# Phase 1 and 2 of a fused attention and ternary FFN kernel: key transposes moved inside the tile, scan of |W| on three buffers

## The chip, the cores and the metric

One Trainium2 chip, eight NeuronCores, one program. The time is device microseconds of the slowest core. Each core owns 8 of the 32 query tiles of one batch element (cores 0 to 3 the first, 4 to 7 the second), and computes keys and values for all 32 tiles of its batch element itself. No core talks to another.

## The reference, cut to what is computed

```python
xn = layernorm(x)                                    # x: [2, 4096, 2048] f32
q, k, v = xn @ Wq.T, xn @ Wk.T, xn @ Wv.T            # 16 heads of 128
q = LN_head(q * gamma + beta) * 128**-0.5            # layernorm over each head
k = LN_head(k * gamma + beta)
attn = tril((q @ k.T) ** 2)
o = (attn @ v) / (attn.sum(-1) + 1e-5)
attn_out = o @ Wo.T
# FFN with ternary weights and int8 activations
wq(w) = clip(round(w / m), -1, 1) * m,  m = mean(|w|)      # over the whole matrix
gate, up = bit_linear(xn, gate_w).split(2)           # gate_w [11264, 2048]
ffn = bit_linear(silu(gate) * up, down_w)            # down_w [2048, 5632]
return x + attn_out + ffn
```

The mean of |w| over each whole FFN matrix is needed before any weight can be made ternary. The kernel gets it by reading both matrices once in 264 chunks of 128x1024 float32 (512 KB) beside the attention's projections; this text calls it the scan.

## The kernel before, in words

The program is written as five in-order instruction lists, one for each engine: `sync` (SP, most DMAs), `gpsimd` (POOL, the casting weight loads and the scan's loads), `tensor` (PE), `vector` (DVE) and `scalar` (ACT). Nothing reorders them: the order in which the Python code calls the helpers is the order in each queue, and an instruction whose semaphore isn't there holds everything behind it on its engine.

**Phase 1** (`for t in range(NT)`, 32 tiles of 128 tokens) makes keys and values. For tile t:
- `pe_transposes` (L339): 16 transposes of the normalized tile `xnb` into two PSUM banks `tp_ps`, four to a bank, copied to `xnT` by ACT (groups 0 and 2, L345) and DVE (1 and 3, L349). The third group needs the bank that ACT's first copy frees.
- `proj_mm(wk_sb)` and `proj_mm(wv_sb)` (L364): 64 matmuls each into the same four banks `kv_ps`, so the V projection can only start in a bank when DVE has read K from it.
- `head_transposes_store` (L418): 16 transposes of the finished keys `kfm`, copied by ACT (L425) and DVE (L429) into two small buffers `ktb` (they are `sgn[0]` and `sgn[1]`; `sgn` in the rows), and stored to `ksc` in 16 DMAs of 32 KB on SP (256 bytes per partition). Groups 2 and 3 wait until the four stores of groups 0 and 1 have landed. Here it is the keys of tile **t-1** that are transposed and stored, between the K and V projections of tile t: `kfm` and `kfm2` form a ring.
- `featuremap_evac` (L374, DVE: K times gamma, PSUM to `kg`), `ln_tile` of tile t+1 (L299 to L322), `featuremap` (L381 to L402: beta, per-head layernorm, ends with 16 small DVE instructions that write `kfm`).
- four ACT copies of V (L480) and 16 stores to `vsc`.
- `emit_abs` (the scan, L283 on ACT, buffer `wfp`): two chunks before the V copies and four after the V stores, so that on ACT six stand together, broken only by the V copies. The load of a chunk is a POOL DMA that waits until the ACT instruction that last read its buffer is done. There are two buffers.
The load of the next tile, `xf`, is on SP, behind the stores of the tile before.

**Phase 2** (`for s in range(NOWN)`, 8 own tiles) makes queries and the int8 activations in the same manner, with 3+3+3 chunks of the scan in each tile. `head_transposes_store` is called twice, for the queries (`qsc`, 16 DMAs of 32 KB) and for the quantized activations (`xqsc`, through `wide_fn`: 4 DMAs of 128 KB, 1024 bytes per partition). Here the keys' ring is already used: tile s-1 is stored after the projection of tile s. Ahead of the next K projection DVE has to get through the quantization (L552 to L573), which starts when ACT's L549 is done; L549 stands behind three chunks of the scan.

**Phase 3** is the attention, and behind it, in the same stretch between barriers, `emit_thresh` turns the sums of the scan into thresholds (L700 to L728, a chain of small DVE and PE instructions). **Phase 4** is the output projection and the FFN. Between phases all engines meet at a barrier.

## Time and profile before

| what | value |
|---|---|
| median of the timed runs | 5087.8 us (5084.0 and 5091.6) |
| profiled execution | 5106.7 us, span of its slowest core 5105.2 us |
| cores of that execution | 5045.9 to 5105.2 us, granted TensorE clock 0.818 to 0.824 of full |
| start until the first projection | 0 to 114 us |
| phase 1 | 114 to 2001 us |
| phase 2 | 2001 to 2592 us |
| phase 3, attention | 2592 to 3543 us |
| thresholds | 3543 to 3551 us |
| phase 4 | 3551 to 5105 us |

Times in the rows are microseconds from the span's start. In a view in order of time a row has the start, the time the group of like instructions took, engine, line, output<-inputs and count; in brackets is how long the engine had been idle and what released it. TensorE's clock is at 1.2 GHz or at 2.4 GHz; the granted clock of a stretch is the mean share of 2.4 GHz.

### The profile page before, as it was taken

The numbers are of one execution on the slowest core, as the hardware profiler recorded it, in microseconds if no ns is written. First come the engines' busy times: TensorE is split into PE (matmuls) and PEld (weight loads), VectorE is DVE, ScalarE is ACT, GpSimd is POOL, SyncE is SP. The second block draws the span as 40 slices with busy tenths as digits, with TensorE's granted clock in tenths as the row PEclk, the third lists the DMA queues.
The fourth block names the chain that finished last, engine by engine and source line by source line (L and its number), as shares of the span: only waits on it lengthen the run. The fifth ranks groups of instructions, "written<-read, shape, count | busy, mean of one in ns | idle before, by whom it ended". The sixth has DMA issues, their size and how long they took to land.

```text
span 5105.2 us, 52147 instructions; the slowest of 8 cores (5045.9 to 5105.2 us)
## 1 busy us (share of the span) xinstructions
PE 3066.7 (60%) x13416; PEld 1270.3 (25%) x13416; DVE 1845.7 (36%) x3416; ACT 1816.3 (36%) x2685; POOL 240.6 (5%) x452
## 2 busy tenths in 40 slices
PE   1665556655556563233346667776889999512789
PEld 0222222222222221111111112221334433201333
DVE  0333333333433342444433312222266666333221
ACT  0222222222322222222334455554144444354551
POOL 1000000000000001000000000000000000000000
PEclk9777777777877876666679899999999999755899
DMA  9333332232233225433221221111466666345886
GB/s 165 83 83 88 92 104 85 83 87 83 88 105 92 85 84 127 113 99 107 91 88 47 56 87 59 65 71 51 120 234 229 232 236 225 122 160 170 248 277 201
DMA packets 312716, 628.19 MB, mean 123 GB/s; under 512 B 181872, under 2 KB 194160, under 8 KB 280432
## 3 DMA queue, kind: packets, MB, share of 16 engines
q0 software_dynamic: 64512, 310.41, 20.2%
q1 hardware_dynamic: 247920, 314.45, 19.9%
q8 instruction: 123, 2.02, 0.2%
q14 instruction: 161, 1.32, 0.1%
HBM read 573.34 MB, written 84.93 MB: 129 GB/s over the span
## 4 chain that ended last, share of the span: by engine, by line
PE 28%; DVE 22%; DMA 18%; ACT 14%; issue 11%; SPq 3%; another core or an unknown queue 2%; DVEq 1%; ACTq 1%; POOLq 0%; POOL 0%
PE kv_ps L364 13%; DMA wfp<-gwt_r 6%; DMA xob<-xown 4%; PE ops L675 3%; SPq L80 3%; ACT s2t L658 3%; DVE s2t L660 2%; DMA hgr<-hgscr 2%; ACT sgn L762 2%; ACT sgn L765 2%; PE zps L679 2%; PE sps L647 2%; PE dps L1138 2%; DVE kg L381 2%
## 5 line engine op out<-in xcount | busy, mean ns | idle before, releaser
L364 PE MATMUL kv_ps<-wk_sb,xnT 128*128 128x512 bf16 x2560 | 644.3, 419 | 159.9 <-DMA wv_sb<-wvt 84.8
L364 PE MATMUL kv_ps<-wv_sb,xnT 128*128 128x512 bf16 x2048 | 517.3, 420 | 176.2 <-DVE kg L374 176.2
L339 PE MATMUL tp_ps<-ident,xnb 128*128 128x128 bf16 x640 | 69.5, 272 | 835.3 <-ACT xnT L345 691.4
L675 PE MATMUL ops<-s2t,vsb 128*128 128x512 bf16 x768 | 302.4, 394 | 285.1 <-DVE s2t L660 233.3
L660 DVE TENSOR_TENSOR s2t<-s2t,msk_sb 128x512 bf16<-128x512 bf16 x512 | 217.3, 424 | 630.0 <-ACT s2t L658 625.4
L658 ACT ACTIVATE s2t<-sps 128x512 bf16<-128x512 f32 x512 | 305.8, 597 | 316.8 <-PE sps L647 306.3
L283 ACT ACTIVATE sgn<-wfp 128x1024 bf16<-128x1024 f32 x264 | 279.1, 1057 | 343.7 <-DMA wfp<-gwt_r 190.5
L364 PEld LDWEIGHTS kv_ps<-wk_sb,xnT 128*128 128x128 bf16 x2560 | 267.4, 106 | 527.8 <-issue 284.1
L913 PE MATMUL gps<-terng,xqs 128*128 128x512 bf16 x1408 | 343.8, 401 | 74.0 <-DVE ternu L781 57.4
L1138 PE MATMUL dps<-dtern,hqts 128*128 128x512 bf16 x1408 | 330.7, 398 | 72.9 <-DMA hqts<-hqtd 66.4
L425 ACT COPY sgn<-tp_ps 128x512 bf16<-128x512 bf16 x96 | 56.3, 586 | 793.3 <-PE tp_ps L418 621.2
L364 PEld LDWEIGHTS kv_ps<-wv_sb,xnT 128*128 128x128 bf16 x2048 | 214.9, 106 | 468.5 <-issue 274.5
L429 DVE COPY sgn<-tp_ps 128x512 bf16<-128x512 bf16 x96 | 40.8, 425 | 782.7 <-PE tp_ps L418 532.0
L647 PE MATMUL sps<-qsb,ksb 128*128 128x512 bf16 x768 | 303.4, 397 | 28.5 <-DMA qsb<-qsc 28.4
L925 PE MATMUL ups<-ternu,xqs 128*128 128x512 bf16 x1408 | 318.3, 379 | 0.0
L679 PE MATMUL zps<-s2t,ones_bf 128*128 128x512 bf16 x768 | 304.2, 396 | 0.0
L339 PEld LDWEIGHTS tp_ps<-ident,xnb 128*128 128x128 bf16 x640 | 51.7, 121 | 860.0 <-issue 860.0
L675 PEld LDWEIGHTS ops<-s2t,vsb 128*128 128x128 bf16 x768 | 74.5, 97 | 560.4 <-issue 559.1
L913 PEld LDWEIGHTS gps<-terng,xqs 128*128 128x128 bf16 x1408 | 143.2, 102 | 262.1 <-issue 113.2
L374 DVE TENSOR_TENSOR kg<-kv_ps,gmb 128x512 f32<-128x512 f32 x160 | 110.7, 692 | 268.1 <-PE kv_ps L364 235.9
L1138 PEld LDWEIGHTS dps<-dtern,hqts 128*128 128x128 bf16 x1408 | 141.3, 102 | 262.0 <-issue 115.0
L1066 PE MATMUL tp<-ident,hgb 128*128 128x128 bf16 x352 | 51.5, 301 | 244.3 <-DVE hgb L1042 173.9
(138 smaller groups left out, 3542.3 us busy)
## 6 DMA issues: line engine op xcount, KB each, us to landing
wfp<-gwt_r POOLq DMA_DIRECT2D x176, 512.0 KB, 4.9
wfpt<-gwt_r POOLq DMA_DIRECT2D x88, 1024.0 KB, 5.2
wfp<-dwt_r POOLq DMA_DIRECT2D x88, 512.0 KB, 4.2
xqs<-xqsc SPq DMA_DIRECT2D x88, 512.0 KB, 3.9
wfpt<-dwt_r POOLq DMA_DIRECT2D x44, 1024.0 KB, 8.0
hqts<-hqtd SPq DMA_DIRECT2D x32, 1408.0 KB, 8.9
xf<-xfull SPq DMA_DIRECT2D x32, 1024.0 KB, 7.1
hgscr<-hgb SPq DMA_DIRECT2D x88, 256.0 KB, 2.1
```

What stands on the lines that cost most here:

```text
L80: return self.op(engine, lambda e, o=out, i=in_: e.dma_start(out=o, in_=i), waits=waits, inc=sem, inc_n=16)
L283: lambda e, sl=slot, t=tgt, cc=col: e.activation(wabs_dump[:], wfp[sl][:], ACT.Abs, accum_out=t[:, cc:cc + 1]), waits=[s_abs[slot]]))
L339: TE(lambda e, bb=bank, f=fc, jj=j, s=src_bf: e.transpose(bb[:, jj * 128:(jj + 1) * 128], s[:, f * 128:(f + 1) * 128], ident[:]), waits=wl ...
L364: TE(lambda e, jj=j, f=fc, w=w_sb: e.matmul(kv_ps[jj][:], xnT[:, f * 128:(f + 1) * 128], w[:, f * DM + jj * 512: f * DM + (jj + 1) * 512], ...
L647: TE(lambda e, sl=slot, vv=v, bb=sb: e.matmul(sps[bb][:], ksb[sl][:, vv * 128:(vv + 1) * 128], qsb[sl][:], start=True, stop=True), waits=w ...
L658: sck = SC(lambda e, bb=sb: e.activation(s2t[bb][:], sps[bb][:], ACT.Square), waits=[(cT, mm_ck)])
L660: vck = V(lambda e, bb=sb, vv=v: e.tensor_tensor(s2t[bb][:], s2t[bb][:], msk_sb[:, (vv % 16) * 512:((vv % 16) + 1) * 512], ALU.mult), wait ...
L675: TE(lambda e, sl=slot, vv=v, bb=sb, hh=h, n=NC: e.matmul(ops_[hh % 2][:], vsb[sl][:, vv * 128:(vv + 1) * 128], s2t[bb][:], start=(vv == 0 ...
L679: TE(lambda e, vv=v, bb=sb, hh=h, n=NC: e.matmul(zps[hh % 2][:], ones_bf[:], s2t[bb][:], start=(vv == 0), stop=(vv == n - 1)), inc=(v == N ...
L913: TE(lambda e, f=fc, r=ring, bb=pb, xs=xslot: e.matmul(gps[bb][:], xqs[xs][:, f * 128:(f + 1) * 128], terng[r][:, f * 512:(f + 1) * 512], ...
L925: TE(lambda e, f=fc, r=ring, bb=pb, xs=xslot: e.matmul(ups[bb][:], xqs[xs][:, f * 128:(f + 1) * 128], ternu[r][:, f * 512:(f + 1) * 512], ...
L1138: TE(lambda e, f=fc, h_=hs, bb=pb, r=ring: e.matmul(dps[bb][:], hqts[h_][:, f * 128:(f + 1) * 128], dtern[r][:, f * 512:(f + 1) * 512], st ...
```

## The change

1. In phase 1 the keys of tile t are transposed and stored in iteration t itself: behind the V projection, `ln_tile` and `featuremap`, ahead of the V copies. `kfm2` is not used in phase 1 any more.
2. The scan has three buffers `wfp` instead of two, and its six chunks of a tile stand in three pairs: behind the copies to `xnT`, behind `featuremap`, and behind the V stores. In phase 2 the places are as before.
3. The stores of the quantized activations in phase 2 are 16 DMAs of 32 KB instead of 4 of 128 KB. The layout in DRAM is the same.
4. The thresholds are computed behind phase 2, between two barriers, instead of behind the attention.
5. Every one of the 16 V stores has its wait written out; `lnz` is in another buffer; an unused semaphore and an unused branch go.

```diff
-    wfp = [E(nc.sbuf_tensor(f"wfp{i}", [128, 1024], F32)) for i in range(2)]
+    wfp = [E(nc.sbuf_tensor(f"wfp{i}", [128, 1024], F32)) for i in range(3)]
-    lnz = kg
+    lnz = wfp[0]
...
-            slot = i % 2
+            slot = i % 3
...
         kck = proj_mm(wk_sb, first_waits=[(s_w, ck_winit)] + xnT_ready)
-        if pend1[0] is not None:
-            pfm = pend1[0]
-            head_transposes_store(kfm_ring[(t - 1) % 2], pfm,
-                                  lambda h, tt=t - 1: ksc[h, :, tt, :])
-            kfm_free2[(t - 1) % 2] = [(cT, cT.n)]
+        emit_abs(2)
         featuremap_evac(kck)
         vck_banks = proj_mm(wv_sb, first_waits=[])
...
-        fm_ck = featuremap(kfm_ring[slot], q_scale=False,
-                           dst_waits=kfm_free2[slot])
-        pend1[0] = fm_ck
+        fm_ck = featuremap(kfm, q_scale=False,
+                           dst_waits=st["kfm_free"])
         emit_abs(2)
+        kt_ck = head_transposes_store(kfm, fm_ck,
+                                      lambda h, tt=t: ksc[h, :, tt, :])
+        st["kfm_free"] = [(cT, kt_ck)]
         for j in range(4):
             v = SC(lambda e, jj=j, xs=slot: e.copy(
...
-                  s_kvw[slot], waits=([(cS, sck)] if h == 0 else []))
+                  s_kvw[slot], waits=[(cS, sck)])
         st["xnb_free"][slot] = [(s_kvw[slot], s_kvw[slot].n)]
         emit_abs(2)
-        emit_abs(2)
-    head_transposes_store(kfm_ring[(NT - 1) % 2], pend1[0],
-                          lambda h: ksc[h, :, NT - 1, :])
...
-            head_transposes_store(xnb[pslot], pqb, None,
-                                  wide_fn=lambda g, ss=s - 1:
-                                  xqsc[ss].rearrange("p f c -> p (f c)")
-                                  [:, g * 512:(g + 1) * 512])
+            head_transposes_store(xnb[pslot], pqb,
+                                  lambda fc, ss=s - 1: xqsc[ss, :, fc, :])
...
     b.wait("sync", s_ktb[0], s_ktb[1], s_kvw[0], s_kvw[1])
+    b.barrier(bar)
+    emit_thresh(wabs_g, N_GW, thg_p, thg_m, hmg, 176)
+    emit_thresh(wabs_d, N_DW, thd_p, thd_m, hmd, 88)
...
     b.barrier(bar)
```

The order of TensorE in phase 1 before, from one K projection on (`kfm` are the keys to be transposed, `xnb` the normalized tile):

```order
L364 MATMUL kv_ps<-wk_sb,xnT 128x512 x64
L418 MATMUL tp_ps<-ident,kfm 128x128 x16
L364 MATMUL kv_ps<-wv_sb,xnT 128x512 x64
L339 MATMUL tp_ps<-ident,xnb 128x128 x16
L364 MATMUL kv_ps<-wk_sb,xnT 128x512 x64
```

and with the change:

```order
L354 MATMUL kv_ps<-wk_sb,xnT 128x512 x64
L354 MATMUL kv_ps<-wv_sb,xnT 128x512 x64
L408 MATMUL tp_ps<-ident,kfm 128x128 x16
L329 MATMUL tp_ps<-ident,xnb 128x128 x16
L354 MATMUL kv_ps<-wk_sb,xnT 128x512 x64
```

The transposes of the keys moved from between the two projections to behind them, and are now those of the same tile. The order of ScalarE in phase 1 before, from the end of one tile's feature map on (`sgn<-wfp` is the scan, `xnb<-kv_ps` the V copies, `sgn<-tp_ps` the copies of transposed keys):

```order
L395 ACTIVATE st<-st 128x16
L283 ACTIVATE sgn,wabs_g<-wfp 128x1024 x2
L480 CAST xnb<-kv_ps 128x512 x4
L283 ACTIVATE sgn,wabs_g<-wfp 128x1024 x4
L345 COPY xnT<-tp_ps 128x512 x2
L425 COPY sgn<-tp_ps 128x512 x2
L299 ACTIVATE xnb,lnst<-xf 128x2048
```

and with the change:

```order
L385 ACTIVATE st<-st 128x16
L273 ACTIVATE sgn,wabs_g<-wfp 128x1024 x2
L415 COPY sgn<-tp_ps 128x512 x2
L459 CAST xnb<-kv_ps 128x512 x4
L273 ACTIVATE sgn,wabs_g<-wfp 128x1024 x2
L335 COPY xnT<-tp_ps 128x512 x2
L273 ACTIVATE sgn,wabs_g<-wfp 128x1024 x2
L289 ACTIVATE xnb,lnst<-xf 128x2048
```

Of the four chunks between the V copies and the copies to `xnT` two stay, and two now stand behind the copies to `xnT`.

## Rows read from the trace of the kernel before

**Rows 1.** The stretches of the program, busy time of each engine (first row: columns).

```profile
core 5: us, PE busy (x) PEld busy (x) DVE busy (x) ACT busy (x) POOL busy (x), PEclk, DMA share, GB/s
...
114.00:2001.00 1887.00, 1116.13 (x5104) 499.14 (x5104) 663.14 (x1239) 504.08 (x793) 102.27 (x190) 0.79 0.31 88
2001.00:2592.50 591.50, 175.51 (x896) 84.67 (x896) 259.62 (x432) 163.21 (x256) 48.30 (x88) 0.62 0.39 109
...
3543.00:3552.00 9.00, 1.48 (x8) 1.22 (x8) 3.27 (x20) 0.00 (x0) 0.92 (x2) 0.53 0.00 1
```

**Rows 2.** Who waited for whom from 160 to 1960 us: us, times, longest.

```profile
PE tp_ps L339 <- ACT xnT L345: 513.1, 31, 20.8
...
ACT sgn L283 <- DMA wfp<-gwt_r: 188.4, 111, 7.0
PE kv_ps L364 <- DVE kg L374: 170.5, 30, 6.1
```

**Rows 3.** TensorE in order of time, one tile of phase 1 from K to K.

```profile
1003.02 16.11 PE L364 MATMUL kv_ps<-wk_sb,xnT 128*128 128x512 bf16 x64 [0.96 <-DVE xnT L349]
...
1026.53 16.30 PE L364 MATMUL kv_ps<-wv_sb,xnT 128*128 128x512 bf16 x64 [5.63 <-DVE kg L374]
...
1061.70 1.87 PE L364 MATMUL kv_ps<-wk_sb,xnT 128*128 128x512 bf16 x4 [0.96 <-DVE xnT L349]
```

**Rows 4.** ScalarE in order of time, the same tile.

```profile
1019.55 0.59 ACT L425 COPY sgn<-tp_ps 128x512 bf16<-128x512 bf16 x1 [17.18 <-PE tp_ps L418]
1023.24 0.59 ACT L425 COPY sgn<-tp_ps 128x512 bf16<-128x512 bf16 x1 [3.10 <-DMA ksc<-sgn]
...
1045.58 2.60 ACT L480 CAST xnb<-kv_ps 128x512 bf16<-128x512 f32 x4
...
1057.77 1.06 ACT L283 ACTIVATE sgn<-wfp 128x1024 bf16<-128x1024 f32 x1 [2.36 <-DMA wfp<-gwt_r]
...
1059.01 0.59 ACT L345 COPY xnT<-tp_ps 128x512 bf16<-128x512 bf16 x1
```

**Rows 5.** VectorE in order of time, the same tile.

```profile
1028.87 2.29 DVE L302 TENSOR_REDUCE lnst<-xf 128x1 f32<-128x2048 f32 x1
...
1034.44 2.29 DVE L381 TENSOR_TENSOR kg<-kg,btb 128x2048 f32<-128x2048 f32 x1
...
1043.53 4.19 DVE L402 TENSOR_SCALAR kfm<-kg,st 128x128 bf16<-128x128 f32 x16
```

**Rows 6.** TensorE in order of time, tile 0.

```profile
113.98 16.88 PE L364 MATMUL kv_ps<-wk_sb,xnT 128*128 128x512 bf16 x64 [84.75 <-DMA wv_sb<-wvt]
130.70 13.98 PE L364 MATMUL kv_ps<-wv_sb,xnT 128*128 128x512 bf16 x64
```

**Rows 7.** VectorE in order of time, tile 0, the row behind the last read of K.

```profile
131.92 2.29 DVE L302 TENSOR_REDUCE lnst<-xf 128x1 f32<-128x2048 f32 x1
```

**Rows 8.** SP's queue in order of time, the tile of rows 3.

```profile
1020.21 7.41 SPq L80 DMA_DIRECT2D ksc<-sgn  x16
1048.25 7.92 SPq L80 DMA_DIRECT2D vsc<-xnb  x16
1056.32 0.43 SPq L80 DMA_DIRECT2D xf<-xfull  x1
```

**Rows 9.** DMA issues of phase 1: count, KB each, median us to landing.

```profile
wfp<-gwt_r POOLq DMA_DIRECT2D x170, 512.0 KB, 4.9
...
ksc<-sgn SPq DMA_DIRECT2D x496, 32.0 KB, 1.5
vsc<-xnb SPq DMA_DIRECT2D x496, 32.0 KB, 3.0
```

**Rows 10.** Phase 2, all engines in order of time, behind one tile's feature map.

```profile
2344.46 4.41 SPq L80 DMA_DIRECT2D xqsc<-sgn  x4
...
2364.96 4.19 DVE L402 TENSOR_SCALAR kfm<-kg,st 128x128 bf16<-128x128 f32 x16
...
2370.39 1.06 ACT L283 ACTIVATE sgn<-wfp 128x1024 bf16<-128x1024 f32 x1 [3.75 <-DMA wfp<-dwt_r]
...
2371.63 1.91 ACT L549 ACTIVATE kg<-xn_f 128x2048 f32<-128x2048 f32 x1
...
2373.80 0.15 DVE L552 TENSOR_SCALAR lnst<-lnst 128x1 f32<-128x1 f32 x1 [4.65 <-ACT kg L549]
```

More of the change, by code:

```diff
@@ L270, in emit_abs @@
             src, which, col = abs_chunks[i]
[L271 to L272 removed]
+            slot = i % 3
             b.dma("gpsimd", wfp[slot][:], src, s_abs[slot],
[L274 removed]
+                  waits=[(cS, abs_sc_ck[slot])])
             tgt = wabs_g if which == 0 else wabs_d
[L276 to L285 removed]
+            abs_sc_ck[slot] = SC(
+                lambda e, sl=slot, t=tgt, cc=col: e.activation(
+                    wabs_dump[:], wfp[sl][:], ACT.Abs,
+                    accum_out=t[:, cc:cc + 1]), waits=[s_abs[slot]])
     st = {
@@ L433, in head_transposes_store @@
             st["tp_evac"][g % 2] = ck
-            if wide_fn is not None:
-                b.dma("sync", wide_fn(g), ktb[kslot][:, 0:512],
+            for j in range(4):
+                h = g * 4 + j
+                b.dma("sync", dst_fn(h), ktb[kslot][:, j * 128:(j + 1) * 128],
                       s_ktb[kslot], waits=[(CTR[ck[0]], ck[1])])
-            else:
-                for j in range(4):
-                    h = g * 4 + j
-                    b.dma("sync", dst_fn(h), ktb[kslot][:, j * 128:(j + 1) * 128],
-                          s_ktb[kslot], waits=[(CTR[ck[0]], ck[1])])
             st["ktb_free"][kslot] = s_ktb[kslot].n
@@ L446, in build_nc @@
     st["xn_ck"][0] = ln_tile(xf[0], want_f32=False, xslot=0)
-    kfm_ring = [kfm, kfm2]
-    kfm_free2 = [[], []]
-    pend1 = [None]
     for t in range(NT):
@@ L516, in build_nc @@
     pend = [None]
+    kfm_ring = [kfm, kfm2]
+    kfm_free2 = [list(st["kfm_free"]), []]
     for s in range(NOWN):
@@ new lines, in build_nc, with emit_thresh @@
+    assert abs_i[0] == len(abs_chunks), abs_i[0]
+    def emit_thresh(src, n_elems, th_p, th_m, hm, ncols):
+        ngr = ncols // 11
+        V(lambda e, s_=src, ng=ngr: e.reduce_sum(
+            wabs_r.ap()[:, 0:ng].rearrange("p (g o) -> p g o", o=1),
+            s_.ap().rearrange("p (g d) -> p g d", g=ng), axis=AX.X),
+          waits=[(cS, cS.n)])
+        V(lambda e, ng=ngr: e.reduce_sum(wabs_s[:, 0:1], wabs_r[:, 0:ng], axis=AX.X))
+        TE(lambda e: e.matmul(minips[0:1, 0:1], wabs_s[:], onesrf[:],
+                              start=True, stop=True), waits=[(cV, cV.n)])
+        tck = cT.n
+        V(lambda e: e.tensor_copy(mini1[0:1, 0:1], minips[0:1, 0:1]),
+          waits=[(cT, tck)])
+        V(lambda e, n=n_elems: e.tensor_single_scalar(
+            mini1[0:1, 1:2], mini1[0:1, 0:1], 1.0 / n, ALU.mult))
+        V(lambda e: e.tensor_single_scalar(mini1[0:1, 1:2], mini1[0:1, 1:2],
+                                           EPS, ALU.max))
+        vck = V(lambda e: e.tensor_single_scalar(mini1[0:1, 2:3], mini1[0:1, 1:2],
+                                                 0.5, ALU.mult))
+        TE(lambda e: e.matmul(minips[:, 0:2], ones1f[:], mini1[0:1, 1:3],
+                              start=True, stop=True), waits=[(cV, vck)])
+        tck = cT.n
+        V(lambda e, hh=hm: e.tensor_single_scalar(hh[:], minips[:, 0:1], 0.5,
+                                                  ALU.mult), waits=[(cT, tck)])
+        V(lambda e, tp=th_p: e.tensor_copy(tp[:], minips[:, 1:2]))
+        vck = V(lambda e, tm=th_m: e.tensor_single_scalar(
+            tm[:], minips[:, 1:2], -1.0, ALU.mult))
+        return vck
```

65 lines of the change are left out of this document (10 added, 55 removed).

## The prediction

> **What bounds the kernel now.** I read the stretches first [rows 1]. Phase 1 is 1887 of 5105 us, 59 us for each of 32 tiles, with a granted clock of 0.79 and 30% DMA share: TensorE is busy 1116 us and waits the rest. Phase 2 is another 591.5 us, the thresholds stand alone in 9 us. The change touches nothing else. Next, who waited for whom in phase 1 [rows 2]: TensorE loses 513 us in 31 waits (16.5 us a tile) for ScalarE's copy to `xnT`, and 170.5 us in 30 waits (5.7 us a tile) for VectorE's read of K. ScalarE itself waits for scan loads, 188 us in 111 waits, 1.7 us each.
>
> Then one tile in order of time. K runs from 1003.02, V from 1026.53, the next K from 1061.70, a period of 58.7 us [rows 3]. The first hole lies between K and V: the transposes of the old keys stand there, and their last copy on VectorE waits for stores, with the reads of K queued behind it, so V starts 7.4 us after K's end (1019.13 to 1026.53). The second lies behind V's end at 1042.83: ScalarE has two scan chunks, the V copies (1045.58), four more chunks, of which the last begins at 1057.77 after waiting 2.36 us for its load, and only then the copy at 1059.01 that frees the bank for the third group of transposes. K follows 2.69 us later [rows 3, 4]. With two buffers and four chunks in a row, ScalarE runs at the pace of the loads.
>
> **Part 1 and 2, phase 1, worked out as one new tile.** Time 0 is the start of K. The queues are in order, so the new period is a chain whose links I take from the old rows.
> - K takes 16.1 us [rows 3]. V follows at once, since nothing holds VectorE's reads of K now. Tile 0 of before already has that order, as there are no old keys to transpose: V's row has no wait, and takes 13.98 us, not 16.30, because TensorE doesn't fall back to the lower clock between them [rows 3, 6]. V ends at 30.1.
> - VectorE begins the layernorm of the next tile 1.06 us after K's end (130.86 to 131.92) [rows 6, 7]: at 17.2.
> - From there to the end of `kfm` it is 18.85 us (1028.87 to 1047.72) [rows 5]: 36.0. V is hidden under this; TensorE waits 5.9 us.
> - The first group is transposed and ScalarE begins to copy it about 0.85 us later. (An estimate: the 2.69 us from copy to K hold two such steps and two copies, of 0.59 and some 0.4.) 36.9. The scan pair ahead of it takes 2 x 1.24 us (1057.77 to 1059.01 is one) from about 31 on, and is done.
> - The copy of the third group starts 3.69 us behind the first (1019.55 to 1023.24, with 3.10 us of waiting for the stores) [rows 4] and takes 0.6: 41.2.
> - V copies 2.6: 43.8. Scan pair 2.5: 46.4. Both its loads could start as soon as the first pair of this tile and the second one's first chunk were done, over 10 us earlier, against a landing of 4.9 us [rows 9]; so its wait goes. Then 2.7 from the copy to K: **49.1 us**.
> - VectorE's copy of the fourth group comes 1.6 us behind ScalarE's third, at 42.5, and holds nothing: the transposes behind it have until 46.4.
> - The first pair of scan chunks, behind the copies to `xnT`, lies under K, where ScalarE has nothing else.
> - SP: its 16 key stores take 7.41 us, the V stores 7.92, the load of `xf` follows [rows 8]. That puts `xf` 3.5 us into the next tile, needed at 17.2: covered by 13.7 us. The waits written out at the V stores cost nothing, the key stores have the same kind and are issued no slower.
>
> What is new is that the key stores go out while the two loads just asked for by the second pair may still be moving. Rows bound this: key stores land in 1.5 us when alone, V stores, which share their time with scan loads, in 3.0 [rows 9]. So each tile may pay 0 to 1.5 us at the third group. Most of the loads are over by then (asked for at about 33 and 34, landing in 4.9), so I take 0.5: 49.6 us. The Trainium skill ("Trainium Kernel Development and Optimization", Key Constraints) says that DMAs of SP and POOL run on the same 16 engines and interleave. The landing times of rows 9 agree with it; by that rule alone the upper end, 1.5 us, would hold, some 30 us on the total.
>
> Tile 0 has a K of 16.9: 50.4. The last tile has no layernorm of a next one (5.6 us less, 1028.87 to 1034.44 [rows 5]), and ends on SP: keys out at 16.1 + 1.1 + 13.3 + 0.85 + 0.6 = 31.9, then 7.4 and 7.9 of stores and 0.5 for contention: 48. Sum 50.4 + 30 x 49.6 + 48 = 1586 against 1887 [rows 1]: **-301 us**.
>
> **Part 2 and 3, phase 2.** Between feature map and quantization ScalarE has three scan chunks, and the third waits 3.75 us for its load [rows 10]. With three buffers all three were loaded long before. VectorE's L552 would start 3.5 us earlier, since `kfm` ends at 2369.15 and ScalarE's L549 takes 2.1; this chain sets the next K. The stores go against it: 16 of 32 KB are issued at the pace of rows 8, 0.46 us each, 1.85 for a group of four, 7.4 for all, where the four wide ones take 4.4 [rows 8, 10]. The next layernorm is queued behind the last of those copies on VectorE. The copies of the four groups then come 1.9 us apart; from the old order I get 1.4 us more until the last. Bounds: 0 (all hidden) and 3.0 (the whole difference). Net -2.1 a tile for six tiles, -3.5 for the first, which stores nothing, and about nothing for the last, where the stores end the phase: **-16 us**. The Trainium skill ("DMA: Bandwidth & Descriptors", Specifications) says that transfers below 512 bytes are done by read-modify-write. The stores of 256 bytes per partition in rows 9 land in 1.5 us, so I see no such price in the trace. If each of the four groups paid another 1.5 us for it, phase 2 would come out at about +20 instead of -16.
>
> **Part 4 and 5.** The threshold chain is 9 us, alone on the chip before [rows 1] and alone after, since a barrier stands on both sides. One barrier more: no row shows one by itself, between 0 and 2 us, I take 1. The other edits move nothing that anyone waits for.
>
> **Sum.** The profiled execution took 5106.7 us, 1.5 beyond its span. 5106.7 - 301 - 16 + 1 = 4790.7. It is 18.9 us above the median of the timed runs (5087.8), which I take off: **4772 us**, 6.2% less.
>
> **The rivals.**
> - *Contention eats a part.* Key stores land in 3.0 us, and the third scan pair still waits 1.7 us for each load as in rows 2. That is 1.0 + 3.4 = 4.4 us more a tile, 31 x 4.4 = 136: 4908. For it: more bytes in less time, 88 GB/s become 105. Against: before, the DMA engines stand idle through most of K and V.
> - *Slower: ScalarE's queue starves the copies.* All that TensorE needs at a tile's end now hangs on one chain with scan chunks in it. If loads issued beside 32 small stores took so long that each chunk of the third pair waited the 7.0 us that rows 2 have as their longest, the period would grow by 14: 4772 + 31 x 14 = 5206. It breaks even at 10.2 us a tile. Against: the loads are asked for over 10 us ahead.
> - *`xf` late.* It stands behind 32 stores on SP. If it landed after 24 rather than 10 us, the layernorm would hold VectorE 7 to 8 us a tile: about 5010.
> - *The clock.* TensorE is idle or at small transposes for 19 us before each K. Before it was as long (1042.83 to 1061.70), and K began at the lower clock as well (4 matmuls in 1.87 us) [rows 3]. If all of K ran so (0.43 us each, 27.5 us), 31 x 11.4 gives 5125. The trace has no such K.
>
> **How the numbers follow.** Forecast 0.80 (4735 to 4850 by itself), contention 0.12, late `xf` 0.03, starving 0.03, clock 0.02. What a measurement of this kernel can tell from no change is about 2%, 4986 to 5190. Faster 0.92, same 0.05, slower 0.03. The range of 8 in 10 runs from 4725, where the period is 48, to 4885, which takes in the full 1.5 us of contention, the bounds of phase 2 and a part of the first rival.
>
> **What would show each step.** Phase 1 of about 1586 us; K to K near 49.5; V without a wait before it and near 14 us; TensorE waiting some 6 us for `kfm` and no longer for K's reads; no scan chunk behind the V copies waiting for its load; `xf` landed before VectorE is free for it; phase 2 some 16 us shorter, its copies behind `xqsc` 1.9 us apart; the threshold chain at 9 us before the attention. The prediction is wrong if the third scan pair waits for loads, if the copies of keys wait over 5 us for their stores, or if something other than `kfm` releases the key transposes.

## The result, and the profile after

The kernel with the change takes 4803.8 us (median of 11 runs, 4786.0 to 4920.0) against 5092.9 us before, timed in turns with it (10 runs, 5079.7 to 5158.3). The ratio is 0.943, with an interval of 0.9396 to 0.9465. The forecast was 4772 us, a ratio of 0.938 to its own median. The profiled execution took 4816.7 us; its slowest core is core 2 with a span of 4815.1, where the working of the forecast, before its last step to the median, gave 4790.7. In several executions one die shows a lower granted clock than the other and all its cores are longer; these are left out of the ratios and of the medians in the table of experiments.

First the cores, then the stretches of core 2, as in [rows 1].

```profile
core 0: 4783.3 us, clock 0.814
core 1: 4799.2 us, clock 0.816
core 2: 4815.1 us, clock 0.813
...
core 5: 4784.6 us, clock 0.826
core 6: 4754.9 us, clock 0.828
```

```profile
core 2: us, PE busy (x) PEld busy (x) DVE busy (x) ACT busy (x) POOL busy (x), PEclk, DMA share, GB/s
115.10:1705.60 1590.50, 1078.75 (x5009) 509.90 (x5104) 663.15 (x1239) 505.92 (x795) 101.98 (x189) 0.79 0.38 104
1705.60:2291.70 586.10, 170.47 (x889) 85.17 (x904) 263.04 (x452) 163.16 (x256) 48.51 (x88) 0.62 0.40 110
2283.90:2291.70 7.80, 1.48 (x8) 1.22 (x8) 3.39 (x20) 0.00 (x0) 0.00 (x0) 0.50 0.00 0
```

Nearly the whole gain is in the first row: phase 1 went from 1887 us [rows 1] to 1590.5. VectorE and ScalarE do the same work as before (663.15 and 506 us); TensorE waits less, and its busy time falls a little (to 1089 us on core 5; on core 2 some 95 of its records are missing). The second row holds phase 2 and now the thresholds too: 578.3 and 7.8 us, where they were 591.5 and about 8.2.

Core for core it can be set out fully. Core 5, on which the rows of before were read, went from 5105.2 to 4784.6 us, 320.6 less, where the forecast had 316 (301 + 16 - 1). That is 296.6 in phase 1, 13.0 in phase 2 with the thresholds, 1.3 in the attention and 10.4 in phase 4, less 0.7 in the time until the first K. Phase 4 has the same instructions in both kernels; on core 2 it took 12 us *more* than on core 5 before (1566.5 against 1554.2), with a granted clock of 0.81 for 0.85.

Who waited for whom in phase 1 after the change, 160 to 1690 us (us, times, longest):

```profile
ACT xnb L289 <- DMA xf<-xfull: 308.1, 30, 11.8
...
PE tp_ps L408 <- DVE kfm L392: 192.4, 31, 6.7
...
DVE sgn L419 <- DMA ksc<-sgn: 159.9, 30, 7.0
...
ACT sgn L415 <- DMA ksc<-sgn: 102.1, 30, 4.7
...
PE tp_ps L329 <- ACT xnT L335: 98.3, 31, 3.7
PE tp_ps L329 <- ACT sgn L415: 89.1, 30, 4.2
...
PE tp_ps L329 <- DVE sgn L419: 45.0, 30, 3.1
...
ACT sgn L273 <- DMA wfp<-gwt_r: 27.8, 29, 2.3
```

Against [rows 2]: TensorE's wait for the copy to `xnT` fell from 513.1 to 98.3 us, its wait for VectorE's read of K is no longer in the list, and ScalarE's wait for scan loads fell from 188.4 to 27.8. In their place stand 192.4 us for `kfm`, 6.2 a tile, and 89.1 and 45.0 us for the two copies of keys (`sgn`, L415 and L419) that free the banks for the transposes of `xnb`: a part of the old wait for `xnT` now has other names. All waits of TensorE in these two lists add up to 747 us before and 481 after, and that difference of 265, with some 27 us less busy time, is nearly all of the gain of phase 1. The first row is long but ends before anybody needs its result: `xnb` here is only the sum of squares' scratch, and VectorE is not yet free for the next layernorm.

TensorE in order of time, one tile from K to K, to be held against [rows 3]:

```profile
1012.17 16.47 PE L354 MATMUL kv_ps<-wk_sb,xnT 128*128 128x512 bf16 x62 [1.34 <-DVE xnT L339]
...
1028.47 13.98 PE L354 MATMUL kv_ps<-wv_sb,xnT 128*128 128x512 bf16 x63
...
1049.14 1.01 PE L408 MATMUL tp_ps<-ident,kfm 128*128 128x128 bf16 x8 [6.69 <-DVE kfm L392]
...
1063.41 3.19 PE L354 MATMUL kv_ps<-wk_sb,xnT 128*128 128x512 bf16 x7 [1.34 <-DVE xnT L339]
```

V has no bracket, so it waits for nothing, and takes 13.98 us instead of 16.30. The hole is now in one piece, behind V, and is released by `kfm`.

ScalarE and VectorE of the same tile, for [rows 4, 5]; the last row is the `xnT` copy that frees the bank for the third group:

```profile
1029.68 2.29 DVE L292 TENSOR_REDUCE lnst<-xf 128x1 f32<-128x2048 f32 x1
...
1044.70 4.19 DVE L392 TENSOR_SCALAR kfm<-kg,st 128x128 bf16<-128x128 f32 x16
...
1049.92 0.59 ACT L415 COPY sgn<-tp_ps 128x512 bf16<-128x512 bf16 x1 [3.28 <-PE tp_ps L408]
...
1054.49 0.59 ACT L415 COPY sgn<-tp_ps 128x512 bf16<-128x512 bf16 x1 [3.98 <-DMA ksc<-sgn]
...
1055.16 2.60 ACT L459 CAST xnb<-kv_ps 128x512 bf16<-128x512 f32 x4
...
1057.11 0.42 DVE L419 COPY sgn<-tp_ps 128x512 bf16<-128x512 bf16 x1 [6.30 <-DMA ksc<-sgn]
...
1057.86 1.06 ACT L273 ACTIVATE sgn<-wfp 128x1024 bf16<-128x1024 f32 x1
...
1059.10 1.06 ACT L273 ACTIVATE sgn<-wfp 128x1024 bf16<-128x1024 f32 x1
...
1060.33 0.59 ACT L335 COPY xnT<-tp_ps 128x512 bf16<-128x512 bf16 x1
```

Counted from K's start at 1012.17, the links are: layernorm 17.5 (forecast 17.2), end of `kfm` 36.7 (36.0), first key copy 37.8 (36.9), third key copy 42.3 (36.9 + 3.7, with 0.5 for contention 41.1), V copies 43.0, third pair of scan chunks 45.7 (43.8 + 0.5) and without a wait, the `xnT` copy 48.2 (46.4 + 0.5), next K 51.2. VectorE's fourth key copy comes at 44.9, where the forecast had 42.5. This tile is one of the longer ones: the mean from K to K is 49.8 us, the range 48.6 to 51.4, and the forecast 49.6.

The DMA issues of phase 1, for [rows 9], and one tile of SP's queue, for [rows 8]:

```profile
wfp<-gwt_r POOLq DMA_DIRECT2D x173, 512.0 KB, 5.0
xf<-xfull SPq DMA_DIRECT2D x30, 1024.0 KB, 8.0
ksc<-sgn SPq DMA_DIRECT2D x512, 32.0 KB, 1.5
vsc<-xnb SPq DMA_DIRECT2D x511, 32.0 KB, 4.2
```

```profile
1050.58 8.78 SPq L80 DMA_DIRECT2D ksc<-sgn  x16
...
1059.45 7.33 SPq L80 DMA_DIRECT2D vsc<-xnb  x14
```

Key stores still land in 1.5 us, V stores in 4.2 where they took 3.0. `xf` lands in 8.0 us and its queue position is as late as forecast: it was asked for at 1015.54 and was there at 1025.71, 4 us before VectorE is free for it.

Phase 2 behind one tile's feature map, for [rows 10]:

```profile
1912.80 7.75 SPq L80 DMA_DIRECT2D xqsc<-sgn  x16
...
1936.88 1.06 ACT L273 ACTIVATE sgn<-wfp 128x1024 bf16<-128x1024 f32 x1
...
1938.13 1.91 ACT L525 ACTIVATE kg<-xn_f 128x2048 f32<-128x2048 f32 x1
...
1940.30 0.15 DVE L528 TENSOR_SCALAR lnst<-lnst 128x1 f32<-128x1 f32 x1 [0.99 <-ACT kg L525]
```

The third chunk has no bracket: its wait of 3.75 us is gone, and VectorE's L528 stands idle for 0.99 us instead of 4.65. The stores of the activations take 7.75 us in the queue for 4.41, and the four copies behind them (1912.15 to 1917.97) stand 1.9 us apart in the mean, as forecast.

### The profile page after: what moved, and what is told of

Its sections match the earlier page's. It is cut to its first block, busy times and chain, and to the rows that moved or that the text cites. A ratio compares the mean times of both kernels' runs of the same rounds, so it can differ in the third digit from the quotient of the medians.

```text
span 4815.1 us, 52576 instructions; the slowest of 8 cores (4754.9 to 4815.1 us)
## 1 busy us (share of the span) xinstructions
PE 3051.7 (63%) x13164; PEld 1292.5 (27%) x13416; DVE 1846.2 (38%) x3416; ACT 1815.5 (38%) x2685; POOL 241.3 (5%) x452
## 4 chain that ended last, share of the span: by engine, by line
PE 33%; DVE 24%; ACT 15%; issue 11%; DMA 10%; another core or an unknown queue 3%; SPq 3%; DVEq 1%; ACTq 1%; POOL 0%; POOLq 0%
PE kv_ps L354 13%; PE dps L1114 4%; PE ops L685 3%; ACT s2t L668 3%; DVE kfm L392 3%; SPq L80 3%; PE gps L889 3%; DMA hgr<-hgscr 2%; DVE s2t L670 2%; PE sps L657 2%; DMA xob<-xown 2%; PE zps L689 2%; ACT sgn L738 2%; ACT sgn L741 2%
## 5 line engine op out<-in xcount | busy, mean ns | idle before, releaser
L354 PE MATMUL kv_ps<-wk_sb,xnT 128*128 128x512 bf16 x2482 | 629.9, 418 | 182.2 <-DMA wv_sb<-wvt 86.2
L354 PE MATMUL kv_ps<-wv_sb,xnT 128*128 128x512 bf16 x2016 | 445.6, 379 | 1.7
L329 PE MATMUL tp_ps<-ident,xnb 128*128 128x128 bf16 x640 | 86.9, 303 | 540.7 <-ACT xnT L335 234.8
L1114 PE MATMUL dps<-dtern,hqts 128*128 128x512 bf16 x1379 | 370.1, 437 | 36.5 <-DMA hqts<-hqtd 27.8
L354 PEld LDWEIGHTS kv_ps<-wv_sb,xnT 128*128 128x128 bf16 x2048 | 200.4, 98 | 241.6
L408 PE MATMUL tp_ps<-ident,kfm 128*128 128x128 bf16 x640 | 76.0, 289 | 248.5 <-DVE kfm L392 215.7
L1114 PEld LDWEIGHTS dps<-dtern,hqts 128*128 128x128 bf16 x1408 | 152.4, 109 | 253.8 <-issue 238.4
L415 ACT COPY sgn<-tp_ps 128x512 bf16<-128x512 bf16 x96 | 56.3, 586 | 412.9 <-PE tp_ps L408 221.2
```

The lines of the kernel that those rows point to most:

```text
L329: TE(lambda e, bb=bank, f=fc, jj=j, s=src_bf: e.transpose(bb[:, jj * 128:(jj + 1) * 128], s[:, f * 128:(f + 1) * 128], ident[:]), waits=wl ...
L354: TE(lambda e, jj=j, f=fc, w=w_sb: e.matmul(kv_ps[jj][:], xnT[:, f * 128:(f + 1) * 128], w[:, f * DM + jj * 512: f * DM + (jj + 1) * 512], ...
L1114: TE(lambda e, f=fc, h_=hs, bb=pb, r=ring: e.matmul(dps[bb][:], hqts[h_][:, f * 128:(f + 1) * 128], dtern[r][:, f * 512:(f + 1) * 512], st ...
```

## The experiments

Twelve runs were made. The lengths of phase 1 and of phase 2 with the thresholds, from the profiled execution of each (the time from the first K to the load of `gnw_s`, and from there to the load of the attention's mask), are the finest measure, since the phases are apart. They are those of the core that ended last, unless the table says otherwise; K to K is the mean from tile 1 on:

| kernel | phase 1 | phase 2 + thresholds | K to K, phase 1 | median, ratio to before in the same session |
|---|---|---|---|---|
| before (core 5) | 1887.1 | 599.7 | 59.1 | 1 |
| after (core 2) | 1590.5 | 586.1 | 49.8 | 4797.8, 0.943 [0.940, 0.947] |
| two_bufs | 1634.6, low clock; 1589.1 on core 4 | 638.6, low clock | 49.6 on core 4 | 4834.5, 0.943 [0.936, 0.950] |
| tail_four | 1754.5 | 585.8 | 55.0 | 4957.3, one run |
| old_order_spread | 1685.1 | 592.8 (no thresholds) | 52.9 | 4897.7, 0.956 [0.949, 0.963] |
| no_scan_p1 | 1537.3, low clock; 1515.9 on core 0 | 587.8 | 47.4 on core 0 | 4745.7, one run |
| wide_stores | 1592.4 | 579.2 | | 4785.3, one run |
| four_slots | 1528.5 | 564.2 | 47.8 | 4722.4, 0.914 [0.907, 0.922] |
| keys_one_later | 1274.1 | 588.5 | 39.4 | 4487.4, 0.868 [0.863, 0.874] |
| two_bufs_again | 1589.6 | 616.0 | 49.8 | 4826.0, 0.942 [0.934, 0.950] |
| after_again | 1586.4 | 585.4 | 49.7 | 4799.4, 0.938 [0.932, 0.944] |
| keys_later_p2 | 1382.7, low clock | 552.8 | 38.7 to 44.4 | 4560.8, 0.888 [0.881, 0.896] |

The kernels wide_stores, four_slots and keys_one_later were timed on a chip on which at least one die had a clock of 0.78 to 0.81 in all seven executions of before (median 5163.5 us; 5114 to 5121 us in the other three sessions of experiments). Against 5117 us their ratios would be 0.923 for four_slots and 0.877 for keys_one_later. The last two runs, keys_later_same and keys_later_p2_same, stand in a table of their own further down.

### What the third scan buffer does

Everything as in the changed kernel, but with two buffers.

```diff
-    wfp = [E(nc.sbuf_tensor(f"wfp{i}", [128, 1024], F32)) for i in range(3)]
+    wfp = [E(nc.sbuf_tensor(f"wfp{i}", [128, 1024], F32)) for i in range(2)]
-            slot = i % 3
+            slot = i % 2
```

> The changed kernel with two scan buffers instead of three. Theory P (the spread into pairs does the work, not the third buffer): the third pair's loads are asked for when the second pair is done, some 9 us before they are needed, against a landing of 5, so K to K in phase 1 stays at 49.5 to 50.2 us and phase 1 at 1590 us, within 20. In phase 2 three chunks stand together and the third waits again: 2 to 3.5 us more in each of 7 tiles, so phase 2 is 15 to 22 us longer and the total about 0.947 of the kernel before. Theory B (the third buffer is needed): the chunks of the third pair wait 1.7 to 3 us each for their loads, K to K 53 to 56 us, phase 1 over 1690 us, total 0.965 to 0.985 of before.

The ratio of 0.943 is the changed kernel's own. But the profiled execution fell on a low granted clock on all cores over the whole span (0.775 to 0.793), on its slowest core with K at 18.4 us and V at 16.98 from tile 13 on, so most of its stretches can't be compared. Phase 1 of cores 4 and 5 can: their V took 13.98 us in 31 of 32 tiles, and phase 1 1589.1 and 1595.3 us, as with three buffers. The kernel was run again beside the changed kernel on one chip:

> The changed kernel with two scan buffers once more, beside the changed kernel itself on the same chip, since the first look at it ran at a lower TensorE clock throughout. Theory P (third buffer not needed where the chunks stand in pairs): K to K in phase 1 within 0.7 us of the changed kernel's 49.9, K to K in phase 2 up from 64.9 by 2 to 4 us (three chunks together), total 15 to 28 us above the changed kernel. Theory B (it is needed): phase 1 longer by 50 us or more.

> The changed kernel unaltered, to compare the one with two buffers with it on one chip: 0.943 of before as measured, within 0.005.

Phase 1 took 1589.6 us with two buffers and 1586.4 with three; phase 2 with the thresholds 616.0 and 585.4. The waits of phase 2 say where, first with two buffers, then with three:

```profile
ACT sgn L273 <- DMA wfp<-dwt_r: 129.5, 40, 44.0
```

```profile
ACT sgn L273 <- DMA wfp<-dwt_r: 62.3, 23, 45.5
```

In phase 1 ScalarE waits more often for loads as well (92.5 us in 58 waits against 19.3 in 29), but at the pair that lies under K, where nobody waits for it. So the third buffer pays only where three chunks stand together: 31 us in phase 2 between these two cores, 27 in the mean of the eight (613.3 and 586.2), 3.3 a tile, and 27 between the medians. The forecast had written "with two buffers and four chunks in a row, ScalarE runs at the pace of the loads"; the cure for phase 1 was that there are no longer four in a row, not the buffer.

### Which of the two moves makes the gain of phase 1

The order of the change is kept, and the pair that lies under K goes back behind the V stores, so that four chunks stand in the tail:

```diff
         kck = proj_mm(wk_sb, first_waits=[(s_w, ck_winit)] + xnT_ready)
-        emit_abs(2)
...
-        emit_abs(2)
+        emit_abs(4)
```

> The changed kernel, three buffers, but the first pair of scan chunks is moved back, so that four chunks stand between the V copies and the copies to xnT. Theory P: three of the four are loaded ahead (3 x 1.24 us); the fourth's load is asked for only when the first of them is done, and lands 4.9 us later. The copy to xnT comes at about 52 instead of 46.4 us into the tile, K to K 55 us, phase 1 some 170 us longer (1760 us), total 4960 to 4985 us. Theory B (with three buffers the place doesn't matter, only the chunk's own time counts): 2 x 1.24 = 2.5 us more, K to K 52.3 us, phase 1 1667 us.

Phase 1 took 1754.5 us, 55.0 from K to K in the mean (53.9 to 57.7). Two chunks moved out of the tail are worth 164 us, 5.3 a tile: twice 1.24 us of work, and the load for which the fourth chunk waits. In this kernel ScalarE's wait for loads is 78.1 us in 25 waits up to 1500 us, 3.1 each, where the changed kernel has 1.0, and that under K.

The opposite: the kernel of before, with its keys between K and V, its two buffers and wide stores, and only the scan spread into pairs.

```diff
         kck = proj_mm(wk_sb, first_waits=[(s_w, ck_winit)] + xnT_ready)
+        emit_abs(2)
         if pend1[0] is not None:
...
         emit_abs(2)
-        emit_abs(2)
```

> The kernel before with one edit: two of the four scan chunks behind the V copies now stand behind the copies to xnT of the next tile, under K. Two buffers, keys of tile t-1 still transposed between K and V. Theory P: the copy to xnT now waits for two chunks only, which by the old rows run at 1048.51 and 1051.19, so it comes at 1052.5 instead of 1059.01: K to K 52 us instead of 58.7, phase 1 about 1680 us, total 0.960 of before. So two thirds and more of the gain without moving a transpose. Theory O (the order of the transposes is what gains, the holes around V): no more than 2 us a tile, total above 0.985 of before.

Phase 1 took 1685.1 us, 202 of the 297 us of the whole change; in the mean of the eight cores it is 1874 before, 1679 here and 1588 in after_again, that is 195 of 286. So the order of the transposes is worth the other 91 to 95 us, 3 a tile (the third buffer also differs, but is worth nothing in phase 1, as shown above): V starts 7.4 us earlier and is 2.3 us shorter, but the transposes and copies of the keys, some 7 us, now stand in the tail. Taken the other way round, with tail_four (1751 in the mean of its cores) as the step between, the order gives 123 us and the spread of the scan 163: the split depends on which comes first, but the spread is the larger part either way. Phase 2 without the thresholds is 592.8, as before.

### What the scan costs in the tail

The chunks of phase 1 are left out altogether, that is 192 of the 264, so the mean of |W| is taken over too little:

```diff
             slot = i % 3
+            if i < 192:
+                continue
             b.dma("gpsimd", wfp[slot][:], src, s_abs[slot],
```

> The changed kernel without the 192 scan chunks of phase 1, loads and sums both (the thresholds come out of the 72 others). It shows what the scan still costs in phase 1. By my sum only the third pair lies on the chain, 2 x 1.24 us, and contention of its loads with the key stores and xf 0.5 us: K to K 46.6 us, phase 1 about 1495 us. If contention costs more than I took, K to K falls below 46; the key stores' wait at ScalarE's third copy is then clearly under the 3.1 to 4 us of the changed kernel, and xf lands in under 7 us instead of 8 to 10. If the scan were hidden altogether, K to K would stay at 49.7.

On core 4, the last to end, phase 1 took 1537.3 us, 53 less than after. But there and on core 5 the clock was low at first: V took 16.98 us in nine of the first ten tiles and 16.0 in the other. On the six other cores V took 13.98 us in every tile, and phase 1 1512.1 to 1518.4 us. Against the 1588 us of after_again on the same chip that is 72 less, 2.3 us a tile, where I had expected 3.0: 2.5 for the third pair's own time and 0.5 for contention. Most of what is missing is the contention, which is smaller than I took (below). The rows in order of time, from core 4 in a tile with V at 13.98 us, show a part of the rest:

```profile
1032.80 0.59 ACT L417 COPY sgn<-tp_ps 128x512 bf16<-128x512 bf16 x1 [3.08 <-DMA ksc<-sgn]
1033.47 2.61 ACT L461 CAST xnb<-kv_ps 128x512 bf16<-128x512 f32 x4
...
1036.16 0.59 ACT L337 COPY xnT<-tp_ps 128x512 bf16<-128x512 bf16 x1
1036.24 0.42 DVE L421 COPY sgn<-tp_ps 128x512 bf16<-128x512 bf16 x1 [6.21 <-DMA ksc<-sgn]
...
1036.81 1.01 PE L331 MATMUL tp_ps<-ident,xnb 128*128 128x128 bf16 x8 [2.70 <-DVE sgn L421]
```

ScalarE's `xnT` copy now comes straight behind the V copies, but VectorE's copy of the fourth key group waits 6.21 us for its stores, and the transposes of the next tile stand behind it. I had written that this copy "holds nothing". It holds nothing as long as the scan pair is there: in the tile of the changed kernel shown above the transposes behind it were done 2.8 us before those that wait for `xnT`. Without the pair they run together, in some tiles, and that can cost some tenths of a microsecond, not more, since the whole shortfall is 0.7.

The run also settles contention. Without any scan load the copies of the keys wait 3.24 us on ScalarE (87.6 in 27) and 5.0 on VectorE (139.9 in 28), and 3.26 and 5.03 on core 0; with the loads it is 3.40 and 5.33. So the stores' wait is not contention but SP's own pace: four stores at about 0.5 us each, and 1.5 until the last has landed. `xf` lands in 6.4 us here and V stores in 1.6, against 8.0 and 4.2, so the loads do slow the other transfers, though none that is waited for.

### The narrow stores

The changed kernel with the four wide stores of the activations put back.

```diff
-            head_transposes_store(xnb[pslot], pqb,
-                                  lambda fc, ss=s - 1: xqsc[ss, :, fc, :])
+            head_transposes_store(xnb[pslot], pqb, None,
+                                  wide_fn=lambda g, ss=s - 1: ...)
```

> The changed kernel with the four wide stores of the quantized activations of before (128 KB each). By my sum the 16 narrow ones cost 1.4 us in each of six tiles: K to K in phase 2 goes from 64.6 to 63.2 us, phase 2 about 10 us shorter; nothing in phase 1. If narrow rows of 256 bytes had a price of their own beyond the issue (1.5 us a group), it would be 5 us or more a tile, 30 us and more in all. If the copies were hidden, nothing moves.

Phase 1 is unchanged (1592.4). In phase 2 K to K fell from 64.85 to 64.09 us and the stretch by 6.9 from core to core. These are single cores; in the mean of the eight, K to K is 63.9 us against 64.9 in after and 65.0 in after_again, and the stretch 576.8 against 584.8 and 586.2. The narrow stores cost 1.0 to 1.1 us a tile, 8 to 9 us in all, inside the bounds of 0 and 3.0 and somewhat under the 1.4 that I took. It is one execution of this kernel. The Trainium skill ("DMA: Bandwidth & Descriptors", Specifications) has transfers under 512 bytes done by read-modify-write. Going by a price of 1.5 us for each group, which is my assumption and not the page's, the change of phase 2 would have been about +20 us; it was -13, so no such price shows here.

### Taking the copies' wait away

The changed kernel with four buffers of half the size for the transposed keys, laid into the same two:

```diff
-    ktb = [sgn[0], sgn[1]]
+    ktb = [sgn[i // 2][:, (i % 2) * 512:(i % 2 + 1) * 512] for i in range(4)]
...
-            kslot = g % 2
+            kslot = g
```

> The changed kernel with four half-size slots for transposed keys (the same two buffers, cut in two) instead of two, so that no copy waits for a store of the same tile. My chain has 3.1 us of waiting for stores at the third group. It goes, and what is left is the transposes and the bank: ScalarE's third copy comes 1.2 instead of 3.7 us behind its first. Phase 1: K to K 47.2 instead of 49.7 us, 78 us less. Phase 2: eight copies with four slots, some 4 to 5 us a tile less, 30 us. Total 100 to 115 us below the changed kernel, 0.922 of before. Rival: V copies and the scan pair behind them were waiting for something else (their loads or V): then under 1 us a tile, total 0.940 of before.

Phase 1 fell by 62 us to 1528.5 (2 us a tile, expected 78 us), phase 2 by 22 (expected 30). That is 84 us where 100 to 115 were expected; the ratio of 0.914 looks better only by the slower executions of before beside it. ScalarE's third key copy no longer waits for a store; it comes 1.5 us behind the first, as its transposes allow:

```profile
1013.57 0.59 ACT L415 COPY sgn<-tp_ps 128x512 bf16<-128x512 bf16 x1 [3.28 <-PE tp_ps L408]
...
1015.08 0.59 ACT L415 COPY sgn<-tp_ps 128x512 bf16<-128x512 bf16 x1 [0.93 <-PE tp_ps L408]
```

This wait of a kernel for its own stores was in both kernels and costs nothing to remove.

### Taking the keys off the chain

What is left in the changed kernel is that TensorE waits for the keys it has just computed. So the keys of tile t-1 are transposed behind the V projection of tile t (not between K and V, as before), all four copies on ScalarE, with four half buffers, `xf` loaded two tiles ahead, two scan buffers, and four scan chunks under K and two ahead of the feature map's square root:

```diff
-        emit_abs(2)
+        emit_abs(4)
         featuremap_evac(kck)
         vck_banks = proj_mm(wv_sb, first_waits=[])
...
+        if pend1 is not None:
+            kt_ck = head_transposes_store(kfm_ring[1 - slot], pend1,
+                                          lambda h, tt=t - 1: ksc[h, :, tt, :],
+                                          act_only=True)
```

> The changed kernel with the keys of tile t-1 transposed behind V of tile t (TensorE: K, V, old keys, xnT), all four copies on ScalarE, four slots, xf loaded two tiles ahead, the six scan chunks away from the tile's end (four behind the copies to xnT, two between the two square roots), two scan buffers (the third has no room beside the second key buffer). If my reading of the chain is right, what is left between K and K is K 16.1, 1.1, VectorE's 18.9 us to the end of the feature map, and the step to the next K, 3.3: K to K 39.5 us. Phase 1 about 1275 us instead of 1590. Phase 2 some 10 to 30 us less (four slots, but two scan buffers). Total 4440 to 4480 us, 0.875 of before. Rival: the scan's loads, the stores and xf now come in less time and hold something (xf or V stores late, scan chunks under K waiting): K to K 43 to 46 us, total 4560 to 4660. If ScalarE's queue is the bound (V copies behind the key copies), the copy to xnT comes after 37.5 us in the tile and K to K is 41.

The median is 4487.8 us (4479.3 to 4637.9, 5 runs), 0.868 of before, interval 0.863 to 0.874. Phase 1 is 1274.1 us and K to K 39.4, against 1275 and 39.5 worked out. Phase 2 did not get the 10 to 30 us shorter that I expected (588.5 us; by the runs above, two scan buffers cost 27 there and four slots give 22, so these two cancel), and the total of 4440 to 4480 us was missed by 8. The edits went in together; of them only the four half buffers were tried alone, 62 us of the 316 in phase 1. TensorE's rows show the hole behind V closed from 21 us to about 9.5; its two projections take 29.3 us of 39:

```profile
948.00 15.35 PE L355 MATMUL kv_ps<-wk_sb,xnT 128*128 128x512 bf16 x64 [0.96 <-DVE xnT L340]
...
963.18 13.98 PE L355 MATMUL kv_ps<-wv_sb,xnT 128*128 128x512 bf16 x64
...
977.00 0.61 PE L409 MATMUL tp_ps<-ident,kfm 128*128 128x128 bf16 x8
```

The transposes of the keys start with V's end, and the first eight wait for nobody.

Phase 2 of that kernel was then given the wide stores, and the middle three scan chunks of each tile, which stood ahead of the square of the quantization, were moved up to the first three, which lie under a projection:

```diff
-        emit_abs(3)
+        emit_abs(6)
...
-        emit_abs(3)
```

> The kernel with keys one tile later, and in phase 2 the three scan chunks ahead of the square of the quantization moved under the projection, and the wide stores of before. In the trace of the kernel with keys one tile later, VectorE waits 4.3 us in each tile of phase 2 for that square, which stands behind the chunks. It goes: 4.2 us, and 0.8 us for the wide stores as measured: K to K in phase 2 from 64.7 to 59.7 us, seven times, total 30 to 38 us less, 0.861 of before. Rival: six chunks under a projection of 16.5 us at 3 us each hold up the copies of queries behind them on ScalarE; then 1 to 3 us a tile come back and the gain is 10 to 25 us.

Phase 2 with the thresholds fell to 552.8 us, 36 less, as expected (30 to 38). But the median was 4560.8, slower than the kernel without this edit, on another chip, and phase 1, which is the same code in both, took 1382.7 us instead of 1274.1, with tiles of 38.7 to 44.4. Either the chip granted less, or the edit of phase 2 hurt phase 1 in a way that I don't see. So both kernels ran again, together on one chip:

> The kernel with keys one tile later, unaltered, beside its variant with another phase 2 on one chip. In its first trace V took 13.98 us in every tile and K to K was 39.3 us, and phase 1 took 1274 us; the variant, whose phase 1 is the same program, was looked at on another chip, where K took 18.9 and V 17.0 us in most tiles and phase 1 took 1383 us. Theory C (the chip grants less clock, the programs don't differ): here both show the same phase 1, within 15 us, whichever of the two values it is. 0.870 of before at the full clock, up to 0.89 at the lower.

> The variant with phase 2 altered, beside the other on one chip. Theory C: phase 1 the same as the other's within 15 us, phase 2 36 us shorter as in its first trace (552 against 588 us with the thresholds), so the total 30 to 38 us below the other, 0.861 of before at the full clock. Rival D (the variant itself causes the lower clock, through what it does in memory layout or load): its phase 1 is again 80 us or more longer than the other's on this chip, and its total is no better.

Medians were 4573.1 (4 runs) and 4559.0 (5 runs), beside 5122.5 of before; in all nine runs at least two cores had a lower granted clock than the rest. The profiled executions decide it core by core:

| | phase 1 | phase 2 + thresholds | span |
|---|---|---|---|
| keys_later_same, core 2 | 1270.2 | 585.3 | 4458.9 |
| keys_later_p2_same, core 2 | 1271.4 | 548.0 | 4408.8 |
| keys_later_same, core 6 | 1343.9 | 589.8 | 4536.1 |
| keys_later_p2_same, core 6 | 1346.8 | 555.4 | 4515.7 |

Both kernels have the same phase 1 on each of these cores (and on cores 3 and 7), and both are 74 to 75 us longer there on core 6 than on core 2 of the same execution. In phase 1 nothing of the program differs between the two cores; their granted clock does. On cores 0, 1, 4 and 5 the kernel with the second phase 2 is 18 to 22 us longer in phase 1, by one more group of four tiles with V at 16.98 us, so whether it meets the lower clock more often is open. Phase 2 is 37 and 34 us shorter. So the long phase 1 comes from the clock of single cores and not from the edit as such, and by its stages the version with both edits is the best of all. In the totals it didn't gain the 30 to 38 us that were expected: its gain is 14 us in the medians, 0.3%, which these runs can't tell from none, since the core that ends last is one of those with less clock.

## Why the prediction was right

- **Phase 1.** 1586 us forecast, 1590.5 measured, and 1584.4 to 1590.5 on the four cores of the other die. K to K 49.6 and 49.8. V without a wait and 13.98 us long: both as forecast, from tile 0 of before.
- **What releases the key transposes** is `kfm`, 6.2 us a tile against 5.9 forecast.
- **Contention** at the key stores: 0.16 us more for ScalarE's wait and 0.33 for VectorE's with the scan loads than without. I took 0.5; the rival with 1.0 there and 3.4 at the scan pair is out, since the scan's wait is 27.8 us in all and stands at the first pair, under K, in every tile.
- **A sign of being wrong that came and meant nothing.** The prediction was to be wrong if the copies of keys waited over 5 us for their stores. ScalarE's, which is in the chain, waits 3.40 us; VectorE's waits 5.33, but the transposes that it holds back (45.0 us in the list above) are done before the `xnT` copy frees the bank for the next. The sign should have named the first of the two.
- **`xf`** landed in 8.0 us, once 10.2. It had no row of its own before and I had counted on something like 7. The cover of 13.7 us held.
- **The third buffer** was credited to phase 1 with "so its wait goes". There the wait goes by placing; in phase 2 it is worth 27 to 31 us by itself, more than my whole term of 16, because the changed kernel with two buffers is slower there (616.0) than before (599.7).
- **Phase 2**: -16 forecast, -13 measured on core 5 and -12 in the mean of the eight cores. In that mean K to K fell from 67.0 to 64.9, by the 2.1 us worked out, and the first tile by 3.3 (forecast 3.5), so the tiles themselves gave 16. What is missing is ahead of the first tile, which I had not counted: from the load of `gnw_s` to the phase's first projection it is now 64.7 us instead of 61.4. The narrow stores cost 1.0 to 1.1 instead of 1.4, so the wait that went was worth a little less than the 3.5 I took.
- **Thresholds**: 7.8 us alone on the chip, 8.2 before. A wash, with the barrier in it.
- **"Holds nothing"** for the fourth key copy: true for this change. In the tile shown it comes 3.2 us ahead of the `xnT` copy (44.9 and 48.2), where 3.9 was worked out. In no_scan_p1 it is not true for every tile.
- **The total** is 27 us above the forecast (4772 scaled by 5092.9 / 5087.8 to the median of before in these runs is 4777). Where from: the rows of before are those of its slowest core. Its phase 1 took 1887 us, the mean of the four cores of its die 1877 (of all eight 1874); after the change the same four, whose clock is undisturbed, have 1587. So the gain is 290 us when like is held against like, not 301, since a core with the longest phase 1 of before need not be the last one afterwards. Phase 2 gave 4 less than forecast. The other 12 or so were not traced run by run; what the profiled execution shows is that cores with less clock are the last ones: cores 0 and 1 took 1609.3 and 1616.9 us for phase 1, and core 2 lost 12 us in phase 4. Core 5 against core 5, without such a loss, the forecast was met within 5 us (316 and 320.6).

The chain of single links was thus right in size and sign; the step that was off was to subtract a saving read on the slowest core from a median of slowest cores.

## What to carry to other kernels

In queues that run in order, what counts is where work of no urgency stands: two scan chunks moved from the chain under a long projection were worth more (163 to 195 us of 286, by the order of the steps) than the move of the transposes, and the extra buffer bought for them was worth nothing there. A result that is transposed and stored one tile late takes its whole production off TensorE's path, provided that the transposes stand where their copies hold up no other projection. Hold cores of equal clock against each other, in stages and not only in totals: read from the slowest core alone, the scan in the tail would have cost 1.7 us a tile instead of 2.3, and the narrow stores 0.76 instead of 1.0 to 1.1.

## What the hardware showed that I had not expected

**A granted clock between the two levels.** In the run keys_later_same, the windows of K and V on core 6, and below them on core 2 of the same execution (columns as in the first windows above):

```profile
902.63:919.64 17.01, 17.01 (x65) 7.01 (x65) 2.08 (x3) 4.97 (x9) 2.11 (x4) 0.80 0.76 203
919.64:936.70 17.06, 17.06 (x69) 7.22 (x68) 14.11 (x21) 5.69 (x9) 1.05 (x2) 0.81 0.25 83
```

```profile
901.32:917.25 15.93, 15.87 (x62) 6.74 (x63) 2.08 (x3) 5.67 (x10) 2.11 (x4) 0.85 0.89 222
917.25:931.30 14.05, 14.00 (x69) 6.51 (x69) 12.07 (x12) 4.41 (x6) 1.06 (x2) 1.00 0.32 96
```

V has two lengths in this run and no others: 13.98 us with 1.00 granted, at 2.4 GHz throughout, and 16.98 us with 0.81, which is neither 1.2 nor 2.4 GHz; 15 of the 32 tiles of core 6 have the second and none of core 2. (In after, two_bufs and no_scan_p1 a few V between the two lengths, 14.2 to 16.9 us, stand at the edges of such stretches.) TensorE had not been idle ahead of this V, so this is not the fall to the lower level between bursts. The Trainium skill ("TensorE: Matmul & The Clock Gate", Seeing it yourself) describes a limit on peak current that holds a whole die at 13/16 of the clock once three of its cores run dense matmuls. The 0.81 agrees; the whole die does not, and the measurement decides. The long V come in pairs of cores, 0 and 1, 2 and 3, 4 and 5, 6 and 7, and nearly always in the same tiles on both. In keys_later_same cores 6 and 7 have 15 each, cores 4 and 5 of the same die 4 each; in no_scan_p1 cores 4 and 5 have 9 each in their first ten tiles and cores 6 and 7 none; in the changed kernel's profiled execution cores 0 and 1 have 11 each and cores 2 and 3 none. In keys_later_same and keys_later_p2_same they come in groups of four tiles, about 177 us (one group is cut off by the end of the phase), with at least one tile at full clock between them. What sets it off here was not tried. The 14 us between the medians of the last two kernels are smaller than the 74 us that one pair of cores loses by it in phase 1.

**K alternates.** With 1.00 granted for V, K takes about 15.0 to 15.6 us in one tile and 15.9 to 16.8 in the next, in most tiles of the changed kernel and of the one with 39 us tiles; in four_slots (core 1) every K of phase 1 takes 16.1 to 16.7 us. It starts at the lower level each time; how much of it runs there changes from tile to tile. I have no experiment on it.

**A load issued late.** Once in phase 1 POOL was late with two loads and waited for nothing that the profile shows (33.63 us is the time since its last issue, not the delay, which is about 3.3):

```profile
1048.65 1.05 POOL L80 DMA_DIRECT2D wfp<-gwt_r  x2 [33.63 <-issue]
```

The scan chunks that freed the buffers were done at 1045.3 and 1046.5, and VectorE wrote `kfm` from 1044.70 to 1048.89. It cost nothing here, since the first of these chunks is used at 1059.10. Whether VectorE's writes are the reason was not tried.
